# Reading the moving operand of the square layers in 16-byte runs, with tokens mixed between the two layers

## The chip, the cores and the metric

The kernel runs on one core of one Trainium2 chip. The metric is the device time of one execution in microseconds (us); lower is better. A core has TensorE for matrix products (PE in the profile, its weight loads PEld), VectorE (DVE), ScalarE (ACT), GpSimd (POOL) and SyncE (SP), which here issues nearly all DMAs. SBUF is the on-chip memory of 128 partitions, PSUM the small memory into which TensorE writes.

## The reference, cut to what matters

The input x is 32 sequences of 128 tokens with 256 features. A cross attention with a masked context comes first; then this feed-forward block, with a residual around it:

```python
def _L0_ffn_ref(x, w1_w, w1_s, w2_w, w2_s, h1_w, h1_s, h2_w, h2_s, w3_w, w3_s):
    def _tlin(x, w, s):
        return jnp.einsum('bsi,oi->bso', x, w) * s
    h = jax.nn.silu(_tlin(x, w1_w, w1_s)) * _tlin(x, w2_w, w2_s)   # 256 -> 1024, twice
    h = jax.nn.gelu(_tlin(h, h1_w, h1_s), approximate=False)       # 1024 -> 1024, square
    h = jax.nn.gelu(_tlin(h, h2_w, h2_s), approximate=False)       # 1024 -> 1024, square
    return _tlin(h, w3_w, w3_s)                                    # 1024 -> 256
x = x + _L0_xattn_ref(ctx_2048, _layernorm(x), ...)
x = x + _L0_ffn_ref(_layernorm(x), ...)
```

Each token goes through the block by itself. The weights of the block are -1, 0 or 1, and the scales s stand behind the product. So it does not matter in which order the tokens of a tile stand, as long as every element of an intermediate is treated alike and the order is restored before the last product.

## The kernel before

The 32 sequences are worked in 16 tiles of two sequences, T = 256 tokens each (`TILES`, `NB`, `T`). An intermediate of the feed-forward block lies with its features on the partitions: `hAh` and `hAl` are 128 partitions x 8 blocks of features (index k) x 256 tokens. The first 128 tokens of such a row of 256 are one sequence, the last 128 the other. Each activation is held as two parts, a rounded high part (`hAh`, `hBh`, `x2h`) and the rest (`hAl`, `hBl`, `x2l`), both of type float32r, and each product is made with both parts and summed in PSUM. Weights of the block are held as float32r in `W1`, `W2`, `H1`, `H2`, `W3`.

In a tile, TensorE makes in this order: the gate and up products (`gate_up`, four groups q of 0 to 3), the k, q and v projections of a later tile (`project_k`, `project_q`, `project_v`), the first square layer (`middle`, q of 4 to 7), attention, scores and output projection of later tiles (`attend`, `scores`, `out_proj`), the second square layer (`middle`, q of 8 to 11), and the last product (`ffn_out`, line 740). The order is written out by hand in `gates_part` and `middle_part`, and a loop runs over tiles 1 to 12.

The square layers are what the change touches. `middle_steps` works one block of 128 output features: for each of the 8 blocks k of input features it calls `part_product` twice, with the high and with the low part. In `part_product` the weights (128 x 128) are the stationary operand and a whole row of 256 tokens, `part[:, k, :]`, is the moving operand; the result goes to 256 columns of one half of a PSUM bank. That is 8 output blocks x 8 k x 2 parts = 128 matmuls for a square layer of one tile, 256 for both, 4,096 in the kernel. `ffn_group`, for the gate and up products, calls the same `part_product`; these matmuls therefore bear the same line, 627.

The first square layer (q < 8) reads `hAh`, `hAl`, the second reads `hBh`, `hBl`. Behind each group, ScalarE applies the gelu with a scale for each partition (`gelu`, line 863: PSUM to `g`), and VectorE splits `g` into the two parts (`split`, lines 1265 and 1267) for the next layer. The second layer's results are written to `hAh`, `hAl` again, which `ffn_out` reads as stationary operand, 128 tokens at a time, so that its output has tokens on partitions in their true order.

The program holds each of these paths twice: with float32r operands (`general` false) and with plain float32 ones. The weights here are exact in float32r, so the first is executed, the `return` at line 627.

Two more uses of a moving operand matter below. `project_q` reads from tile 3 on (line 496) the tile `xnT` in the order in which a DMA left it: as j, a, i with i of 32 tokens, hence in 8 runs of 32 float32 elements (128 bytes) for 256 columns. For tiles 0 to 2 (line 499) the same product reads `xnT` as one run of 256. Both write 256 PSUM columns.

By the sizes of the tiles allocated ahead of them, `hAh` begins at byte 182,944 of a partition and `hBh` at 199,328, both multiples of 32; `hAl` and `hBl` follow 8,192 bytes behind. Each run of 4 elements of the change begins at a multiple of 16 bytes.

Of the kernel before, what the change touches and what calls it, by code (L numbers as in the profile page):

```python
# [5 lines left out]
F32, F32R, I32 = mybir.dt.float32, mybir.dt.float32r, mybir.dt.int32  # L6
# [7 lines left out]
T = NB * P  # L14
TILES = B // NB
KD, KC, KH = D // P, DC // P, HID // P
# [5 lines left out]
EARLY = 2 * KD  # L22
WARM = 8
PAD = 8
MASKED = -3.0e38


# [13 lines left out]
def program(nc, x, ctxT, mask_row, mask_col, wsT, wvT, wtT, woT, first_rows, second_rows, x_mask_1, w1T, w2T, h1T, h2T,  # L41
            w3T, out):
    st = ExitStack()
    with st:
        def sb(name, shape, dt=F32):
            return st.enter_context(nc.sbuf_tensor(name, shape, dt))
# [56 lines left out]

        sb("pad", [P, PAD])
        x2h, x2l = sb("x2h", [P, KD, T], F32R), sb("x2l", [P, KD, T], F32R)
# [4 lines left out]
        y = sb("y", [P, NB, D])  # L110
# [12 lines left out]
        def mrow_of(a):  # L123
            return mrow_1 if isinstance(a, int) and a == 1 else mrow
# [36 lines left out]
        def mid_bank(f, q):  # L161

            if q in (6, 10) and isinstance(f, int) and (f == TILES - 1 or f in (0, TILES - 2) and q == 6):
                return G[0][:].rearrange("p (h t) -> p h t", h=2)
            return F[q % 2][:]
# [96 lines left out]
        def at(name, tile, k):  # L262

            value = tile * PER[name] + k
            return max(value, 0) if isinstance(value, int) else value
# [25 lines left out]
        def wait_mrow(engine, a):  # L291

            if isinstance(a, int) and a == 0:
                engine.wait_ge(firsts_loaded, 16)
            elif isinstance(a, int) and a == 1:
                engine.wait_ge(x_loaded_1, 16)
            else:
                engine.wait_ge(mrow_loaded, at("mrow_loaded", a - 2, 16))
# [148 lines left out]
        def _(pe):  # L447
            mm = nc.tensor.matmul
# [171 lines left out]
                        ins = mm(G[1][:, j * D:(j + 1) * D], lhsT, WO[:, k, :], start=k == 0, stop=k == 2 * KD - 1)  # L620
                ins.then_inc(o_done, 2)

            def part_product(bank, W, k, cols, part, first, last, general):

                if general:
                    return mm(bank, W[1][:, k, cols], part[:, k, :].bitcast(F32), start=first, stop=last)
                return mm(bank, W[0][:, k, cols], part[:, k, :], start=first, stop=last)  # L627

            def ffn_group(bank, W, cols, hi, lo, general, ready=None):

                kk = W[0].shape[1]
                for k in range(kk):
                    if ready is not None:
                        ready(k)
                    part_product(bank, W, k, cols, hi, k == 0, False, general)
                    ins = part_product(bank, W, k, cols, lo, False, k == kk - 1, general)
                return ins
# [49 lines left out]
            def middle_steps(f, q, half, ks, general):  # L687

                W, hi, lo = ((H1, H1_raw), hAh, hAl) if q < 8 else ((H2, H2_raw), hBh, hBl)
                m = 2 * (q % 4) + half  # L690
                for k in ks:
                    if m == 0 and k % 2 == 0:
                        pe.wait_ge(h_ready, at("h_ready", f, q - 4 + k // 2 + 1))
                    cols = slice(m * P, (m + 1) * P)
                    part_product(mid_bank(f, q)[:, half, :], W, k, cols, hi, k == 0, False, general)
                    ins = part_product(mid_bank(f, q)[:, half, :], W, k, cols, lo, False, k == KH - 1, general)
                if half and ks[-1] == KH - 1:
                    ins.then_inc(mid_done, 1)

            def middle(f, q, half, general):  # L700

                if half == 0 and q in (4, 8) and isinstance(f, int) and f == 0:
                    pe.wait_ge(chunk_cast, EARLY + (q // 4) * KH)
                    if q == 8 and general:
                        pe.wait_ge(raw_loaded, 112)
                if half == 0:
                    middle_bank(f, q)
                middle_steps(f, q, half, range(KH), general)

            def middle_three(f, q, general):  # L710

                three = (q, q + 1, q + 2)
                for ks in (range(4), (4, 5), (6, 7)):
                    for i in three:
                        if ks[0] == 0:
                            middle_bank(f, i)
                        middle_steps(f, i, 0, ks, general)
                for i in three:
                    middle_steps(f, i, 1, range(KH), general)
# [296 lines left out]
        def _(dve):  # L1016
# [28 lines left out]
            def mask_bias(a):  # L1045

                wait_mrow(dve, a)
                V.tensor_scalar(mbias[:], mrow_of(a), 0.0, MASKED, ALU.is_equal, ALU.mult).then_inc(mask_bias_ready, 1)

# [510 lines left out]
```

## Time and profile before

| | us |
|---|---|
| device time, median of 2 runs (907.35 to 907.44) | 907.39 |
| span of the profiled execution | 906.1 |
| TensorE busy in the span | 900.6 (99%) |
| TensorE weight loads busy | 865.1 (95%) |
| VectorE busy | 615.8 (68%) |
| ScalarE busy | 390.9 (43%) |
| GpSimd busy | 76.9 (8%) |

How to read it: the profile records one execution. Its span goes from the first to the last instruction, the device time is 1.3 us more. Busy time is the union of the instructions of an engine; matmuls overlap their neighbours, because each has a record of 0.28 us while a new one starts every 0.12 us. So the mean duration of a matmul is not what it costs; what counts is the distance from one start to the next. The granted clock (1.00 is all of it) is what the chip lets TensorE have of its 2.4 GHz.

### The profile page before, as it was taken

The page shows a single profiled execution, that of the slowest core. Times are in us where ns is not written, and L with a number is a line of the kernel's source. Part 1 is how long each engine was busy: PE and PEld are TensorE (multiplying, and loading weights), DVE is VectorE, ACT ScalarE, POOL GpSimd, SP SyncE. Part 2 cuts the span into 40 slices and gives each one's busy share as a digit, 9 for nine tenths or more (in the row PEclk, how much of TensorE's full clock was granted, in tenths as well). Part 3 has the DMA queues.
Part 4 walks back from the last instruction along what each step waited for, and adds up shares of the span by engine and source line. Part 5 has one row for each costly group of instructions (what it writes and reads, how often), then busy time and mean ns, then how long its engine had stood idle before and what let it go on. Part 6 is the DMA issues. An engine that isn't in the chain of part 4 may idle for free.

```text
span 906.1 us, 20825 instructions
## 1 busy us (share of the span) xinstructions
PE 900.6 (99%) x7600; PEld 865.1 (95%) x7600; DVE 615.8 (68%) x1224; ACT 390.9 (43%) x1100; POOL 76.9 (8%) x101
## 2 busy tenths in 40 slices
PE   9999999999999999999999999999999999999998
PEld 8899999999999999999999999999999999999998
DVE  5887858577585776857667586675857857576453
ACT  5872534435253252623525235253443524355231
POOL 3543000010000100001010010100001000000000
PEclk9999999999999999999999999999999999999999
DMA  9932132412314232142311424113241221303000
GB/s 350 382 114 58 60 88 69 122 52 78 84 46 122 58 98 64 40 122 69 112 45 35 122 69 122 35 50 106 69 122 46 72 84 59 94 24 106 24 13 14
DMA packets 82352, 79.27 MB, mean 87 GB/s; under 512 B 8592, under 2 KB 74896, under 8 KB 82320
## 3 DMA queue, kind: packets, MB, share of 16 engines
q1 hardware_dynamic: 81744, 78.31, 28.2%
q10 hardware_dynamic: 576, 0.52, 0.2%
q8 instruction: 21, 0.34, 0.2%
q14 instruction: 11, 0.09, 0.0%
HBM read 51.55 MB, written 27.26 MB: 87 GB/s over the span
## 4 chain that ended last, share of the span: by engine, by line
PE 96%; DVE 1%; DMA 1%; issue 0%; SPq 0%; POOL 0%; ACT 0%; DVEq 0%; POOLq 0%; ACTq 0%
PE F L627 56%; PE G L627 8%; PE F L740 7%; PE G L620 6%; PE G L478 6%; PE G L514 5%; PE G L496 2%; PE S L531 2%; PE G L603 2%; PE F L514 1%; PE S L467 1%; DMA cT<-ctx_t 0%; DMA p_dram<-pb 0%; DMA pr<-p_dram 0%; DVE pr L1107 0%
## 5 line engine op out<-in xcount | busy, mean ns | idle before, releaser
L863 ACT ACTIVATE g<-F,firsts 128x256 f32<-128x256 f32 x248 | 104.0, 472 | 322.9 <-PE F L627 322.7
L627 PE MATMUL F<-hBh,H 128*128 128x256 f32 x1008 | 239.2, 282 | 0.1
L627 PE MATMUL F<-hBl,H 128*128 128x256 f32 x1008 | 236.2, 279 | 0.0
L627 PE MATMUL F<-hAh,H 128*128 128x256 f32 x976 | 231.7, 282 | 0.0
L627 PE MATMUL F<-hAl,H 128*128 128x256 f32 x976 | 228.8, 279 | 0.0
L627 PEld LDWEIGHTS F<-hBl,H 128*128 128x128 f32 x1008 | 190.0, 189 | 0.4
L627 PEld LDWEIGHTS F<-hBh,H 128*128 128x128 f32 x1008 | 188.9, 187 | 0.6 <-ACT g L863 0.3
L627 PEld LDWEIGHTS F<-hAl,H 128*128 128x128 f32 x976 | 183.9, 188 | 0.3
L627 PEld LDWEIGHTS F<-hAh,H 128*128 128x128 f32 x976 | 183.0, 187 | 1.0 <-ACT sil L856 0.4
L1265 DVE CAST hBh<-g 128x512 fp32r<-128x512 f32 x64 | 28.4, 444 | 118.0 <-ACT g L863 117.8
L891 ACT ACTIVATE pr<-pr,nmx 128x128 f32<-128x128 f32 x240 | 92.7, 388 | 0.2
L1267 DVE TENSOR_TENSOR hAl<-g,hAh 128x512 fp32r<-128x512 f32 x128 | 88.7, 693 | 4.4
L1265 DVE CAST hAh<-g 128x512 fp32r<-128x512 f32 x128 | 54.9, 429 | 43.6 <-ACT g L863 42.5
L1431 POOL TENSOR_TENSOR rs<-ve,neg_half 128x2 f32<-128x2 f32 x15 | 10.4, 693 | 648.6 <-DVE ve L1202 648.6
L627 PE MATMUL F<-x2h,W 128*128 128x256 f32 x256 | 61.5, 280 | 0.0
L627 PE MATMUL G<-x2h,W 128*128 128x256 f32 x256 | 61.4, 280 | 0.0
L627 PE MATMUL F<-x2l,W 128*128 128x256 f32 x256 | 61.3, 279 | 0.0
L740 PE MATMUL F<-W,hAh 128*128 128x256 f32 x256 | 61.3, 281 | 0.0
L627 PE MATMUL G<-x2l,W 128*128 128x256 f32 x256 | 61.3, 279 | 0.0
L740 PE MATMUL F<-W,hAl 128*128 128x256 f32 x256 | 61.2, 280 | 0.0
L863 ACT ACT_TABLE_LOAD x17 | 21.8, 1283 | 76.7 <-PE F L627 76.7
L514 PE MATMUL G<-WV,cT 128*128 128x256 f32 x224 | 50.6, 379 | 0.0
(160 smaller groups left out, 1520.0 us busy)
## 6 DMA issues: line engine op xcount, KB each, us to landing
p_dram<-pb SPq DMA_DIRECT2D x30, 512.0 KB, 3.3
pr<-p_dram SPq DMA_DIRECT2D x120, 128.0 KB, 3.2
H_raw<-h SPq DMA_DIRECT2D x16, 512.0 KB, 13.8
cT<-ctx_t SPq DMA_DIRECT2D x14, 512.0 KB, 3.6
x_dram<-xt SPq DMA_DIRECT2D x28, 256.0 KB, 2.4
out<-y SPq DMA_DIRECT2D x32, 128.0 KB, 1.7
x_in<-x_t SPq DMA_DIRECT2D x15, 256.0 KB, 2.7
x2T<-x_dram SPq DMA_DIRECT2D x60, 64.0 KB, 2.0
```

The source lines that it names most:

```text
L478: ins = mm(k_part(a, c), WK[:, k, c * P:(c + 1) * P], cT_of(a)[:, k, :], start=k == 0, stop=k == KC - 1)
L496: ins = mm(to.rearrange("p (j a i) -> p j a i", j=NB, a=ROWS), WQ[:, k, c * P:(c + 1) * P], turned(xnT)[:, :, k].rearrange("p a j i -> p j ...
L514: ins = mm(v_bank(a)[:, j * D:(j + 1) * D], cT_of(a)[:, k, j * P:(j + 1) * P], WV[:, k, :], start=k == 0, stop=k == KC - 1)
L531: ins = mm(S[:, r, j, c, :], qT[rows, c, j * P:(j + 1) * P], kT[rows, c, j * P:(j + 1) * P], start=True, stop=True)
L603: ins = mm(to.rearrange("p (t b) -> p t b", t=ROWS), v[:, j, h * DH:(h + 1) * DH], pT[j][:, :, r * KD + c, :], start=True, stop=True)
L620: ins = mm(G[1][:, j * D:(j + 1) * D], lhsT, WO[:, k, :], start=k == 0, stop=k == 2 * KD - 1)
L627: return mm(bank, W[0][:, k, cols], part[:, k, :], start=first, stop=last)
L740: ins = mm(F[j][:, 0, :], lhsT, W3[:, k, :], start=first, stop=last)
L863: fn(g[:, q % 2, m, :], mid_bank(f, q)[:, m, :], ACT.Gelu, scale=scols[:, col:col + 1]).then_inc(gelu_ready, 1)
L891: ins = fn(pr[j][:, r, c, :], pr[j][:, r, c, :], ACT.Exp, bias=nmx[:, j, h:h + 1], scale=SCALE, accum_out=den[:, j, h:h + 1])
L1265: V.tensor_copy(hi[:, pair, :], g[:, q % 2, :, :]).then_inc(hi_ready, 1)
L1267: V.tensor_tensor(lo[:, pair, :], g[:, q % 2, :, :], hi[:, pair, :].bitcast(F32), ALU.subtract).then_inc(h_ready, 1)
```

## The change

The two square layers read the same 256 tokens of the same row, in another order. The constant `RUN` = 4 is new. In the first square layer the row is seen as 2 halves (b) of 32 runs (a) of 4 elements (c), and read as a, b, c: 4 tokens of the first half, 4 of the second, the next 4 of the first, and so on, with a step of 512 bytes between halves. The PSUM columns are written in order, so that in `g`, `hBh` and `hBl` the tokens of both sequences alternate in groups of 4. In the second square layer the row is seen as 32 pairs (a) of 2 runs (b) of 4 elements, and read as b, a, c: every other run of 16 bytes, first the even ones, then the odd ones. This puts the tokens back into their true order. Each of the 4,096 matmuls of the square layers thus has a moving operand of 64 runs of 16 bytes in place of one run of 1,024 bytes. The PSUM operand is rearranged to the same shape, but its addresses stay consecutive. The number of instructions, their order, the waits, the DMAs, the work of the other engines and the gate and up products stay as they are.

```diff
+RUN = 4
...
-            def part_product(bank, W, k, cols, part, first, last, general):
+            def part_product(bank, W, k, cols, part, first, last, general, order=None):
+                moving = part[:, k, :]
+                if order is not None:
+                    moving = moving.rearrange(order, a=T // (2 * RUN), b=2)
+                    bank = bank.rearrange("p (x y c) -> p x y c", x=moving.shape[1], y=moving.shape[2])
                 if general:
-                    return mm(bank, W[1][:, k, cols], part[:, k, :].bitcast(F32), start=first, stop=last)
-                return mm(bank, W[0][:, k, cols], part[:, k, :], start=first, stop=last)
+                    return mm(bank, W[1][:, k, cols], moving.bitcast(F32), start=first, stop=last)
+                return mm(bank, W[0][:, k, cols], moving, start=first, stop=last)
...
             def middle_steps(f, q, half, ks, general):
                 W, hi, lo = ((H1, H1_raw), hAh, hAl) if q < 8 else ((H2, H2_raw), hBh, hBl)
+                order = "p (b a c) -> p a b c" if q < 8 else "p (a b c) -> p b a c"
...
-                    part_product(mid_bank(f, q)[:, half, :], W, k, cols, hi, k == 0, False, general)
-                    ins = part_product(mid_bank(f, q)[:, half, :], W, k, cols, lo, False, k == KH - 1, general)
+                    part_product(mid_bank(f, q)[:, half, :], W, k, cols, hi, k == 0, False, general, order)
+                    ins = part_product(mid_bank(f, q)[:, half, :], W, k, cols, lo, False, k == KH - 1, general, order)
```

## Rows read from the trace of the kernel before

**Rows 1.** The page's head and first part: busy time, share, instructions of each engine

```profile
span 906.1 us, 20825 instructions
## 1 busy us (share of the span) xinstructions
PE 900.6 (99%) x7600; PEld 865.1 (95%) x7600; DVE 615.8 (68%) x1224; ACT 390.9 (43%) x1100; POOL 76.9 (8%) x101
```

**Rows 2.** Granted TensorE clock of the core, and waits of TensorE in all

```profile
core 0: 906.1 us, clock 1.000
...
PE G L603 <- DMA pr<-p_dram: 1.1, 2, 0.8
PE F L814 <- DVE upd L1372: 1.1, 1, 1.1
```

**Rows 3.** The page's part 4: the chain that ended last, by engine and line

```profile
PE 96%; DVE 1%; DMA 1%; issue 0%; SPq 0%; POOL 0%; ACT 0%; DVEq 0%; POOLq 0%; ACTq 0%
PE F L627 56%; PE G L627 8%; PE F L740 7%; PE G L620 6%; PE G L478 6%; PE G L514 5%; PE G L496 2%; PE S L531 2%; PE G L603 2%; PE F L514 1%; PE S L467 1%; DMA cT<-ctx_t 0%; DMA p_dram<-pb 0%; DMA pr<-p_dram 0%; DVE pr L1107 0%
```

**Rows 4.** The chain in order of time, one tile: start, length (us), line, matmul records

```profile
320.86 1.87 PE F L627 x16
322.73 3.45 PE G L478 x16
326.18 1.73 PE G L496 x8
327.91 3.45 PE G L514 x16
331.36 14.93 PE F L627 x128
346.29 1.01 PE G L603 x32
347.30 1.10 PE S L531 x32
348.40 3.65 PE G L620 x16
352.05 14.94 PE F L627 x128
366.99 3.78 PE F L740 x32
```

**Rows 5.** Timeline of TensorE: q projection with one run, between its neighbours

```profile
46.92 1.89 PE L499 MATMUL G<-xnT,WQ 128*128 128x256 f32 x8
48.64 0.38 PE L514 MATMUL G<-WV,cT 128*128 128x256 f32 x1
```

**Rows 6.** Groups of TensorE, shapes apart: count, busy us, mean ns, idle before

```profile
L627 PE MATMUL F<-hBh,H 128*128 128x256 f32 x1008 | 239.2, 282 | 0.1
L627 PE MATMUL F<-hAh,H 128*128 128x256 f32 x976 | 231.7, 282 | 0.0
L627 PE MATMUL G<-hAh,H 128*128 128x256 f32 x48 | 11.6, 280 | 0.0
L627 PE MATMUL G<-hBh,H 128*128 128x256 f32 x16 | 3.9, 278 | 0.0
```

**Rows 7.** Timeline of weight loads in the second square layer: each start is one load

```profile
299.77 0.19 PEld L627 LDWEIGHTS F<-hBh,H 128*128 128x128 f32 x1
...
300.94 0.19 PEld L627 LDWEIGHTS F<-hBh,H 128*128 128x128 f32 x1
```

**Rows 8.** The costliest groups behind the square layers on ScalarE and VectorE

```profile
L863 ACT ACTIVATE g<-F,firsts 128x256 f32<-128x256 f32 x248 | 104.0, 472 | 322.9 <-PE F L627 322.7
L1267 DVE TENSOR_TENSOR hAl<-g,hAh 128x512 fp32r<-128x512 f32 x128 | 88.7, 693 | 4.4
L1265 DVE CAST hBh<-g 128x512 fp32r<-128x512 f32 x64 | 28.4, 444 | 118.0 <-ACT g L863 117.8
```

## The prediction, made before the changed kernel ran

> **What bounds the kernel now.** I read the head of the page first: TensorE is busy for 900.6 of 906.1 us, the next engine for 68% [rows 1]. Then the clock and TensorE's waits: the granted clock is 1.000, which is the 2.4 GHz level, and the two waits listed come to 2.2 us [rows 2]. So nobody keeps TensorE waiting, and its clock has nothing to regain. The chain of waits says the same from the other side: 96% of what sets the end is TensorE work, 56% under line 627 into bank F alone [rows 3]. A busy TensorE only tells that matmuls overlap, so the view that prices them is the chain in order of time, with the length of each stage and its number of records [rows 4]. The first square layer of a tile is the stage of 128 matmuls at 331.36, 14.93 us long; the second is the stage at 352.05, 14.94 us. The next stage starts where each ends. That is 14.94/128 = 116.7 ns from start to start. The two layers of 16 tiles are 16 x (14.93 + 14.94) = 478 us, 53% of the span. Whatever one changed matmul costs more is paid 4,096 times with nothing over it: 1 ns is 4.1 us, or 0.45%.
>
> The count 4,096 is that of the groups: with the high parts alone 1,008 + 16 in the second layer and 976 + 48 in the first, 2,048 in all, and as many with the low parts [rows 6].
>
> **What a matmul is limited by today.** 256 columns at 2.4 GHz are 106.7 ns. The float32 products show how near a stream comes to that: each makes two records, and 16 of them in a row take 3.45 us, 215.6 ns a record, so that 107.8 ns for 256 columns is the pace if a record streams its columns twice (my reading of 215.6 against 2 x 106.7) [rows 4]. The float32r matmul takes 116.7 ns, 8.9 ns more. Weight loads start at the same distance: ten of them in 300.94 - 299.77 = 1.17 us, 117 ns each [rows 7]. The rows do not tell whether the load or the moving operand sets the 116.7. The gate and up stage with other tiles has the same 1.87/16 = 116.9 ns, the last product, with weights and moving operand from other places again, 3.78/32 = 118.1 ns [rows 4]. So the distance hardly depends on where the operands lie: 1.4 ns is the largest difference seen.
>
> **The change part by part.** It removes nothing and adds no instruction, wait or DMA. The gelu and the split work on whole rows with one scale per partition, whatever the order of the tokens, so their cost stays. The result is written to consecutive PSUM columns as before. The gate, up and last products are not touched. What is left is one price, p: what 64 runs of 16 bytes in place of one run of 1,024 bytes add to the distance of 116.7 ns. The change is worth 4,096 x p.
>
> No row shows p, since no moving operand in this trace has runs of 16 bytes. The nearest is the q projection. It reads 8 runs of 128 bytes from tile 3 on and one run before. The stage with 8 runs takes 1.73 us for 8 records, 216.3 ns each; its neighbours with one run take 3.45/16 = 215.6 ns [rows 4]; the same product with one run takes 48.64 - 46.92 = 1.72 us, 215.0 ns [rows 5]. The difference of 0.7 to 1.3 ns is what the rounding to 0.01 us makes of 8 records. Over 8 runs it is 0.16 ns a run at the most, and could be nothing. These rows have two weaknesses: their matmuls need 256 elements in 216 ns, half the pace of the float32r ones, and a run in them is 8 times longer. They speak against a fixed cost of restarting the address pattern, and say little on whether the memory delivers 16 useful bytes at a time fast enough.
>
> Bounds. Below: if the 8.9 ns over a bare stream were due to the order of reading and all went away, p = -8.9 ns, -36 us. Against it speaks that 116.7 ns is the same for different tiles, which looks like a property of the pair of load and matmul. Above, by cost per run: 64 x 0.16 = 10.2 ns, of which 8.9 ns may be hidden if the load sets the pace (p = 1.3 ns, +5 us), or none (+42 us). Above, by pace: if each 16-byte run costs as much as 32 bytes, 256 columns take 2 x 107.8 = 215.6 ns, p = 98.9 ns, +405 us for both layers. I take p = 0: it is the value to which the q projection is nearest, and a contiguous row must also be fetched piece by piece, so that the number of useful bytes fetched per matmul is the same; only a piece wider than 16 bytes, or a preference for neighbouring pieces, makes a difference. The runs begin at multiples of 16 bytes, so none straddles two such pieces.
>
> The trace shows 8 non-contiguous runs at 216.3 against 215.6 ns [rows 4]. The Trainium skill (Advanced Engine Details and Errata, SBUF Cachelines) says that SBUF has lines of 16 bytes and that a line needs at least two hits for full performance. Each line gets four hits here, so that by the page the sum would be the same 907 us, as with p = 0. No row of this trace tests a line of that size.
>
> Sum: 906.1 + 4,096 x 0 + 1.3 (the median less the span) = 907.4 us. Nothing comes late, so no stall moves. If p were positive, TensorE would only be later everywhere; ScalarE waits 322.9 us in front of the gelus already and VectorE 118.0 us in front of the split of `hBh` [rows 8], so these engines would wait longer, and no other bound would appear. That also means that no slack elsewhere covers p.
>
> **The rivals.**
> Both layers at half pace, 0.13. The memory delivers pieces of 32 bytes or more to TensorE, and a run of 16 bytes uses half of one. Both orders waste the other half: the first layer leaves for the other half of the row, the second steps over it. 907.4 + 405 = 1,312 us. For it: the float32r stream is the fastest reader in this kernel, 1,024 bytes in 107.8 ns, and its need has no reserve in any row. Against it: the rows with 128-byte runs, weakly.
>
> The Trainium skill says of PSUM that any non-contiguous pattern slows matmuls significantly (Advanced Engine Details and Errata, PSUM Cachelines). The PSUM side stays contiguous here; carried over to reading, the rule would be this rival. The q projection, at 216.3 against 215.6 ns, does not follow it [rows 4].
>
> One layer only at half pace, 0.11. Either the second (a step of 32 bytes always meets the same part of an interleaved memory) or the first (a jump of 512 bytes at each run, two places open at once). 2,048 x 98.9 = 203 us, 1,110 us. Nothing in the rows speaks for either; it decides as soon as the delay is over 8.9 ns or, if there is no reserve, over 0.
>
> A bubble at each run, 0.07. One period of 0.42 ns (2.4 GHz) x 64 = 26.7 ns, less 8.9 of reserve or none: p = 17.8 to 26.7, +73 to +109 us. One of 0.83 ns: p = 44 to 53, +182 to +218 us. So 980 to 1,125 us. The 0.16 ns a run above speaks against it.
>
> Faster, 0.03. The alternation relieves a collision between the reads of moving operand and weights; in full -36 us, 871 us. It passes 2% from p = -4.4 ns on. Against it is the equal distance across tiles.
>
> No effect, because the operand is read through a buffer or the load sets the pace: that is inside the forecast. The forecast itself, p between -1.4 and +4.5 ns (-6 to +18 us), has 0.66.
>
> **How the numbers follow.** Most likely 907.4 us; that case's own range is 901 to 926 us. 2% of 907.4 is 18 us, about what a measurement of this kernel can tell from no change: faster ends at 889, slower starts at 926. Faster 0.03, within 2% 0.66, slower 0.13 + 0.11 + 0.07 = 0.31. To hold 8 in 10 the range must take in a part of the slow cases: up to 1,115 us it holds the forecast, the one-layer case and nearly all bubbles, and leaves out both layers at half pace and the gain, 0.16 together. Low end: 900 us, the forecast's 6 us of gain and a little noise.
>
> **What would show it.** In the chain in order of time the two stages of 128 matmuls stay at 14.9 us. If both read 27.6 us, it is the half pace; if one does, its order names the cause. 17.2 to 18.4 or 20.6 to 21.8 us is a bubble at each run. The stages of the gate, the projections and the last product keep their lengths in every case; if they changed, the price would not be in the moving operand. In the group table the idle time before the gelus grows by about what the square layers gain in length. A granted clock below 1.000 would make the forecast wrong in a way that no step here considers.

## The result, and the profile after

The changed kernel takes 928.75 us (928.5 to 928.99, 2 runs) against 907.39 us. The ratio is 1.0235 with an interval of 1.0205 to 1.0265: slower, by a little more than 2%. The forecast was no change, 907.4 us.

The chain of waits of the changed kernel in order of time, one tile (start, length in us, engine and line, matmul records), answers to [rows 4]:

```profile
326.54 1.87 PE F L632 x16
328.41 3.45 PE G L479 x16
331.86 1.73 PE G L497 x8
333.59 3.45 PE G L515 x16
337.04 16.21 PE F L632 x128
353.25 1.01 PE G L604 x32
354.26 1.10 PE S L532 x32
355.37 3.65 PE G L621 x16
359.02 15.08 PE F L632 x128
374.10 3.78 PE F L746 x32
```

Two stages changed and no other. The first square layer, which reads in turn from both halves, went from 14.93 to 16.21 us, from 116.6 to 126.6 ns a matmul. The second, which reads every other run, went from 14.94 to 15.08 us, from 116.7 to 117.8 ns. Gates, projections, attention and last product have the lengths they had. Over 16 tiles this is 16 x (1.28 + 0.14) = 22.7 us; the span grew by 21.1 us, from 906.1 to 927.2.

Most of the missing 1.6 us went into a wait that the first longer stage covered. TensorE's waits before had 1.1 us for a DMA that brings `pr` [rows 2]; both fall in the first pass over the tiles, at 68.7 and 70.2 us. The same list of the changed kernel (engine, line, what it waited for: us, times, longest) has no such row:

```profile
PE F L820 <- DVE upd L1378: 1.1, 1, 1.1
PE F L551 <- DVE pr L1161: 0.3, 1, 0.3
```

The page of the changed kernel, head and busy times, and the group of the gelus with count, busy us, mean ns and the idle time before it, answer to [rows 1] and [rows 8]:

```profile
span 927.2 us, 20825 instructions
## 1 busy us (share of the span) xinstructions
PE 922.6 (100%) x7600; PEld 887.3 (96%) x7600; DVE 617.1 (67%) x1224; ACT 390.6 (42%) x1100; POOL 76.2 (8%) x101
...
L869 ACT ACTIVATE g<-F,firsts 128x256 f32<-128x256 f32 x248 | 104.1, 472 | 338.7 <-PE F L632 338.5
```

VectorE and ScalarE did the same work in the same time: the gelus took 472 ns in both kernels, and ScalarE only waited 15.8 us longer in front of them. The granted clock was 1.000 as before. So the loss is the pace of TensorE in the two stages.

### The profile page after: what moved, and what is told of

Its sections match the earlier page's. It is cut to its first block, busy times and chain, and to the rows that moved or that the text cites. A ratio compares the mean times of both kernels' runs of the same rounds, so it can differ in the third digit from the quotient of the medians.

```text
span 927.2 us, 20825 instructions
## 1 busy us (share of the span) xinstructions
PE 922.6 (100%) x7600; PEld 887.3 (96%) x7600; DVE 617.1 (67%) x1224; ACT 390.6 (42%) x1100; POOL 76.2 (8%) x101
## 4 chain that ended last, share of the span: by engine, by line
PE 98%; DVE 1%; issue 0%; ACT 0%; DVEq 0%; ACTq 0%
PE F L632 59%; PE G L632 8%; PE F L746 7%; PE G L621 6%; PE G L515 5%; PE G L479 5%; PE G L497 2%; PE S L532 2%; PE G L604 2%; PE S L468 0%; PE F L820 0%; DVE mx L1130 0%; DVE pr L1123 0%; PE G L500 0%; PE S L500 0%
## 5 line engine op out<-in xcount | busy, mean ns | idle before, releaser
L632 PE MATMUL F<-hAh,H 128*128 128x256 f32 x976 | 250.9, 295 | 0.0
L632 PE MATMUL F<-hAl,H 128*128 128x256 f32 x976 | 248.3, 292 | 0.0
```

What stands on the lines that cost most here:

```text
L632: return mm(bank, W[0][:, k, cols], moving, start=first, stop=last)
```

## The experiments

All are read by the length of the two stages of 128 matmuls in the chain in order of time, in a tile of the loop. Divided by 128 it is the distance from one matmul to the next. The lengths repeat from tile to tile within 0.02 us, unless the text says otherwise. Each run's kernel is the changed kernel with the edit shown; only the last one is the kernel before with its edit. Each was run once, the last one four times. The granted clock was 1.000, in the run with single elements and in the last one 0.998 on the average: it read 0.96 between 60 and 100 us and 1.00 in all later stretches, where the stages shown lie.

Four theories are asked about first. A: TensorE pays for each jump back, where the outer loop of the address pattern moves on. B: it pays for the distance between one run and the next. C: the price belongs to the place in the tile. D: the reads of weights and of the moving operand collide.

### Does the price belong to the order or to the layer

The row is split into x parts of y runs and read in turn from the parts, y times. 2 parts are the order of the first layer of the changed kernel, 32 parts that of the second, and the run swaps them:

```diff
-                    moving = moving.rearrange(order, a=T // (2 * RUN), b=2)
+                    moving = moving.rearrange("p (x y c) -> p y x c", x=order, c=RUN)
...
-                order = "p (b a c) -> p a b c" if q < 8 else "p (a b c) -> p b a c"
+                order = 32 if q < 8 else 2
```

> The two orders change places: the first square layer reads every other run (step 32 bytes), the second reads in turn from both halves of the row (step 512 bytes); the result is the same. In the changed kernel the stages of 128 matmuls took 16.21 us (126.6 ns each) in the first layer and 15.08 us (117.8 ns) in the second. If the price belongs to the order (theory A or B), the first stage takes 15.08 us and the second 16.21 us, span 927. If it belongs to the place in the tile, to what other engines do meanwhile or to the buffers hA (theory C), they stay at 16.21 and 15.08 us.

Measured, the chain in order of time:

```profile
337.77 15.07 PE F L632 x128
352.85 1.01 PE G L604 x32
353.86 1.10 PE S L532 x32
354.96 3.65 PE G L621 x16
358.61 16.23 PE F L632 x128
```

The two lengths changed places to 0.02 us, and the device time was 930.35 us. The price belongs to the order of reading. What else goes on in the tile, which buffer is read and which weights are loaded have no part in it: theory C is out.

### Jumps back, or distance

The next three runs keep 64 runs of 16 bytes in each matmul. Two have other numbers of parts, and the other layer undoes the order:

```diff
+                    moving = moving.rearrange("p (x y c) -> p y x c", x=order, c=RUN)
...
+                order = 4 if q < 8 else 16
```

and in the second run:

```diff
+                order = 8 if q < 8 else 8
```

> The row is seen as 4 quarters of 16 runs, the first layer reads in turn from the four quarters (steps of 256 bytes, 15 jumps back); the second undoes it (16 parts of 4 runs, steps of 64 bytes, 3 jumps back). Still 64 runs of 16 bytes in each matmul. Theory A, a price for each jump back or change of the outer index (31 of them cost 9.9 ns, 0.32 ns each): 116.7 + 4.8 = 121.5 ns, 15.55 us in the first layer, 117.7 ns, 15.06 us in the second. Theory B, a price for each far step: the first layer has 48 steps of 256 bytes and 15 of 752, no fewer than before, so 126 ns, 16.2 us; the second, with 64-byte steps, between 15.08 and 16.2 us.

> The row is seen as 8 parts of 8 runs and both layers read in turn from the 8 parts (steps of 128 bytes, 7 jumps back), which undoes itself. Theory A: 116.7 + 7 x 0.32 = 118.9 ns, 15.2 us in both layers. Theory B: as many steps of 128 bytes as the first layer of the changed kernel has of 512, so well above 15.2 us in both, up to 16.2, if 128 bytes are far.

The third keeps the nest of loops of the first layer, 32 steps of 16 bytes and in each a pair of runs, but brings the pair near. Each bracket is [step, count] in elements of 4 bytes, the outermost loop first:

```diff
+                moving = bass.AP(moving.tensor, moving.offset, [moving.ap[0], *order])
...
+                order = [[4, 32], [8, 2], [1, 4]] if q < 8 else [[4, 32], [32, 2], [1, 4]]
```

> Both square layers read 32 pairs of runs of 16 bytes, as the first layer of the changed kernel does, with the same 32 steps of 16 bytes of the outer index, but the two runs of a pair lie only 32 bytes apart in the first layer and 128 bytes apart in the second, instead of 512. Some tokens are read twice and others not at all, so the output is not the reference's; the work is the same. Theory A (price for each jump back or change of the outer index): both layers at 126.6 ns, 16.2 us. Theory B (price for distance): the first near 117.8 ns, 15.1 us, the second between that and 16.2 us.

Measured, the stages of 128 matmuls. The run with 4 and 16 parts:

```profile
339.58 17.09 PE F L632 x128
...
362.44 14.69 PE F L632 x128
```

The run with 8 parts in both layers:

```profile
340.13 16.24 PE F L632 x128
...
362.13 15.82 PE F L632 x128
...
397.84 15.83 PE F L632 x128
```

The run with near pairs:

```profile
335.01 15.47 PE F L637 x128
...
356.25 15.37 PE F L637 x128
```

Neither theory holds. In ns a matmul: 2 parts 126.6, 4 parts 133.5, 8 parts 123.6 or 126.9, 16 parts 114.8, 32 parts 117.8, and as pairs 512 bytes apart 126.6, 128 bytes apart 120.1, 32 bytes apart 120.9. With 4 parts there are half as many jumps back as with 2, and the price is higher, so theory A is out. With near pairs it lies between the values of A and B, but the nearer pair is no cheaper than the farther, and 32 parts with steps of 32 bytes cost less than pairs at 32 bytes, so distance alone is out too. Two things were not expected. Eight parts have two lengths for the same instructions, 15.83 and 16.24 us, in turn from tile to tile in the first layer; the second layer, with the same order, always has the shorter. What alternates was not found. And 16 parts, 114.8 ns, are faster than one run, 116.7 ns: the one run of the kernel before is no floor.

### Collisions with the weight load

Two runs ask for theory D. In the first, the square layers' weight loads read one element over and over; in the second, the moving operands lie 32 bytes lower and the weights stay.

> Each weight load of the square layers reads one and the same element of a partition 128 times (step 0) in place of 128 elements; the output is not the reference's, the number and shape of instructions stays. The first layer reads its moving operand as one run (116.6 ns in the kernel before), the second in turn from four quarters, steps of 256 bytes, as the first layer of the run with 4 and 16 parts did (133.5 ns there). Theory D, the reads of weights and of the moving operand collide in the memory and the order only changes how often: both layers come to one distance, near the 107.8 ns of the bare stream, 13.8 us a stage. Theory E, the moving operand alone pays for its far steps: the first layer 14.9 us as before or a little less, the second still about 2.1 us longer than the first.

```diff
+                weights = bass.AP(weights.tensor, weights.offset, [weights.ap[0], [0, P]])
...
+                order = [[1, 256]] if q < 8 else [[4, 16], [64, 4], [1, 4]]
```

> The changed kernel with the pad of 32 bytes ahead of x2h taken out, so that all moving operands of the block (x2h, x2l, hA, hB) lie 32 bytes lower, at a multiple of 64 in place of 32 over one, while the weights stay. Theory D with parts of the memory chosen by low address bits: the stages differ from 16.21 and 15.08 us in at least one layer by over 0.1 us. Theory E: both stay.

```diff
-PAD = 8
+PAD = 0
...
-        sb("pad", [P, PAD])
```

The run with fixed weights, second layer of one tile and first layer of the next two:

```profile
305.32 17.15 PE F L639 x128
...
342.36 15.36 PE F L639 x128
...
400.52 14.52 PE F L639 x128
```

The second and third rows are the first layer, with one run. It has two lengths in turn from tile to tile, as the eight parts had: of the 13 stages of the chain seven took 15.36 us (120.0 ns) and six 14.51 or 14.52 us (113.4 ns). Their mean, 14.97 us, is within 0.04 us of the 14.93 us with real weights. The layer with four parts took 17.15 us, 134.0 ns, against 133.5 with real weights. A weight load that always reads the same element does not remove the cost, so theory D in its plain form is out: most of what the four parts cost does not depend on which addresses the weight load reads. But the one run became 3.4 ns slower in some tiles and 3.3 ns faster in others, so the addresses that the weight load reads are not without effect: with one run a collision of some kind is not excluded.

The run without the pad, a stage of 16 gate products and the two layers:

```profile
321.87 1.92 PE G L631 x16
...
338.18 16.20 PE F L631 x128
...
360.15 15.08 PE F L631 x128
```

With all moving operands 32 bytes lower, at multiples of 64, the two changed layers stayed at 16.20 and 15.08 us, as theory E expected, by which the moving operand alone pays. But the gate products, which read one run, went from 1.87 to 1.92 us for 16, from 116.9 to 120.0 ns. So where a single run starts matters by 3 ns a matmul, and the two orders of the change do not feel it. Whether its own address matters or its place against the weights is open: with fixed weights a single run took the same 120.0 ns in seven stages at its old address.

The two lengths also say how far a comparison of orders carries. One order, and even one run, can differ by up to 6.6 ns a matmul for a reason that was not found. The 126.6 ns of 2 parts and 117.8 ns of 32 were met in both layers, and 4 parts twice at 133.5 and 134.0 ns; 16 parts and each of the near pairs have only one layer of one run.

### What sets 116.7 ns, the load or the columns

> Both square layers read their moving operand as one run, of 224 columns in the first and 128 in the second in place of 256; the remaining tokens are left out, so the output is not the reference's. If the weight load alone sets the 116.7 ns: both stages stay at 14.9 us. If the stream of columns does: 224/256 and 128/256 of it, 102 and 58 ns, 13.1 and 7.5 us. If a load needs about as long as 256 columns do (107 ns) and the rest of 116.7 ns is collision: 107 to 112 ns in the second layer, 13.7 to 14.3 us, whatever the columns.

```diff
+                order = [[1, 224]] if q < 8 else [[1, 128]]
```

```profile
325.59 14.28 PE F L637 x128
...
345.64 14.24 PE F L637 x128
```

224 columns take 111.6 ns and 128 columns 111.2 ns. At both sizes the pair of weight load and matmul needs this distance: the floor. It is not a cost of issuing a pair, for the 32 of line 603, with weight loads of 32 columns, take 1.01 us, 31.6 ns each [rows 4]. With 256 columns in one run the distance is 116.7, 5 ns above the floor. So in the kernel before it is the moving operand that sets the pace, and nothing that is added to its reading is hidden. By its numbers this is the third case of the expectation, 13.7 to 14.3 us whatever the columns. Its reason, that the rest of 116.7 ns is a collision with the load, is not shown, and the next run speaks against a collision paid once a load.

The next run tells whether this is paid for each matmul or for each column. Each matmul gets 512 columns. The first layer reads two whole rows of `hA`; the second reads pairs of runs 512 bytes apart, which covers three quarters of two rows of `hB`, some of it twice:

```diff
+                    moving = part[:, k - k % 2, :]
...
+                order = [[1, 512]] if q < 8 else [[4, 64], [128, 2], [1, 4]]
```

> Each matmul of the square layers reads 512 columns, two rows of hA or hB, and writes both halves of the bank: twice the work on other tokens' columns, so the output is not the reference's. The first layer reads one run of 512; the second reads runs of 16 bytes in turn from two places 512 bytes apart, as the first layer of the changed kernel does, 128 runs. If the 8.9 ns over the bare stream of 256 columns, and the 10.0 ns that this order added, are paid once for each matmul: 222 to 225 ns in the first layer (28.5 to 28.8 us), 232 to 235 in the second (29.7 to 30.1 us). If they are paid for each run or piece: 233 ns (29.9 us) and 253 ns (32.4 us).

The chain, second layer of one tile and first of the next:

```profile
348.81 31.58 PE F L638 x128
...
400.28 29.87 PE F L638 x128
```

One run of 512 columns takes 233.4 ns, twice 116.7. The 8.9 ns over the bare stream of 256 columns are therefore no fixed cost of a matmul; they are its pace, 0.456 ns a column. This pace is that of a run with these weights and addresses, since with fixed weights some stages were faster (113.4 ns for 256 columns). The pairs take 246.7 ns, 13.3 more for 128 runs, where 64 runs cost 10.0 more: neither once a matmul nor quite in proportion. This part fits neither of the two expectations (the two kernels' rows do not have the same places, which may be why).

### Shorter runs

> Runs of one element (4 bytes) in place of 4: the first layer reads in turn one element from each half of the row, the second every other element (step 8 bytes); the result is the same. If memory is fetched in pieces of 16 bytes of which each access of another piece costs a fetch, the first layer makes 256 fetches in place of 64: the column pace halves at least, over 213 ns, 27 us or more; the second makes two hits on each piece, 128 fetches: between 15 and 27 us. If the order of the bytes matters only through collisions with the weight load: both between 14.7 and 17.1 us.

```diff
-RUN = 4
+RUN = 1
...
+                    moving = moving.rearrange("p (x y c) -> p y x c", x=order, c=RUN)
...
+                order = 2 if q < 8 else 128
```

```profile
194.56 14.29 PE F L632 x128
208.86 1.01 PE G L604 x32
209.87 1.10 PE S L532 x32
210.97 3.65 PE G L621 x16
214.62 29.29 PE F L632 x128
```

This is the most telling pair. Single elements taken in turn from two places 512 bytes apart take 111.6 ns, the floor: faster than one run, and 15.0 ns faster than 16-byte runs from the same two places. Single elements with a step of 8 bytes take 228.8 ns, twice the pace. So it is not the number of jumps that costs. Neither expectation holds in either layer: fetches wanted 27 us or more in the first and 15 to 27 in the second, collisions 14.7 to 17.1 us in both, and it was 14.29 and 29.29 us. The collisions are near in the first layer and far off in the second.

> The first layer reads every other run of 8 bytes (2 elements), in two passes over the row; the second reads single elements with a step of 16 bytes, in four passes. The results are not put in order, so the output is not the reference's. Theory F, TensorE fetches pieces of 16 bytes, at best one in 1.67 ns (64 pieces in 107 ns), and every piece left and met again is fetched again: 128 pieces in the first layer, 228 ns as with every other element, 29.3 us; 256 pieces in the second, 427 to 460 ns, 55 to 59 us. Theory G, two hits on a piece are enough for the full pace and only something about the inner step of 8 bytes cost 228.8 ns: 15 us in the first layer, more in the second.

```diff
+                order = [[2, 2], [4, 64], [1, 2]] if q < 8 else [[1, 4], [4, 64]]
```

The chain, second layer of one tile and first of the next:

```profile
342.19 29.86 PE F L637 x128
...
391.94 29.29 PE F L637 x128
```

Runs of 8 bytes with a step of 16 take 228.8 ns, the same as single elements with a step of 8. Single elements with a step of 16 bytes, which use a quarter of each 16-byte piece, take 233.3 ns and not the 427 that a limit on pieces asks for. Theory F met the first layer (29.3 us) and fails in the second, theory G fails in the first: the pace halves and then stays there.

> The first layer reads element by element in turn from four quarters of the row (step 256 bytes), the second from its eight eighths (step 128 bytes). The results are not put in order, so the output is not the reference's. With two halves the stage took 14.29 us. If TensorE keeps four or more pieces of 16 bytes open: 14.3 us in the first layer; eight: 14.3 us in the second too. Where it keeps fewer than the order needs, each element is a fetch: 256 pieces, 427 to 460 ns, 55 to 59 us.

```diff
+                order = [[1, 64], [64, 4]] if q < 8 else [[1, 32], [32, 8]]
```

```profile
341.17 18.33 PE F L637 x128
...
365.26 28.16 PE F L637 x128
```

Four places in turn, element by element, take 143.2 ns and eight places 220.0 ns. Two places are free (111.6 ns), four are dear, eight come near the half pace. Neither expected value came out.

A rule that fits most of this: it is as if TensorE took two float32r elements at a time, and the elements with even and those with odd numbers in the stream behave like two readers, each of which wants two of its own elements in a row from one 16-byte piece. One run gives each reader exactly two. 16-byte runs in any order do too: 114.8 to 133.5 ns, never the half pace. Singles from two halves give each reader four in a row, and only here is the floor of 111.6 ns reached. A step of 8 bytes, 8-byte runs with a step of 16, and a step of 16 bytes all give one: 228.8, 228.8 and 233.3 ns. Four and eight places give one in a row but return to the same pieces at once, and lie between. The rule says nothing of the differences among 16-byte runs, 114.8 to 134.0 ns, which is where the change's own price lies. It was formed behind the runs and no run was made to break it, so it is an argument and not shown.

The Trainium skill (Advanced Engine Details and Errata, SBUF Cachelines) wants two hits on a 16-byte line for full performance. Taken for the whole stream, the runs differ: a step of 8 bytes has two hits on a line and takes 228.8 ns against 116.7.

### Single elements from both halves in every layer

Here the order that reached the floor is used in the gate, up and both square products of the kernel before, and undone where `g` is written:

> Gate, up and both square layers read their moving operand element by element in turn from both halves of the row (steps of 512 bytes), and the tokens are put back at once: the gelu and the gate times up write g with the same steps. The result is the same. With runs of one element the first square layer took 14.29 us (111.6 ns), the same as with 224 columns, against 14.93 before. If that holds in each place: 14.3 us in both square layers and 1.79 us in place of 1.87 for 16 gate or up products, 5,120 x 5.0 = 26 us less than before, 882 us, ratio 0.971. If the strided writes of g cost ScalarE and VectorE so much that TensorE waits, or if the gain needs the other layer's order, between 890 and 907 us.

```diff
-                moving = part[:, k, :]
...
+                moving = part[:, k, :].rearrange("p (b a) -> p a b", b=2)
+                bank = bank.rearrange("p (a b) -> p a b", b=2)
...
+                    fn(g[:, q % 2, m, :].rearrange("p (b a) -> p a b", b=2),
+                       mid_bank(f, q)[:, m, :].rearrange("p (a b) -> p a b", b=2), ACT.Gelu,
...
+                    V.scalar_tensor_tensor(g[:, q % 2, p % 2, :].rearrange("p (b a) -> p a b", b=2),
...
```

It took 901.11 us (899.87 to 901.89, 4 runs) beside 907.98 us of the kernel before (7 runs, taken together with it), ratio 0.992 with an interval of 0.9903 to 0.9936: 0.8% less, clear of the noise and less than half of the 2% that is called a change here. The chain of one tile, a wait of TensorE, the gelu, and the gate times up in this kernel (lowest, median and highest ns) and, last, in the kernel before (busy us and mean ns):

```profile
331.10 14.29 PE F L629 x128
...
351.16 14.29 PE F L629 x128
365.45 3.95 PE F L742 x32
369.40 1.80 PE G L629 x16
...
371.93 0.66 DVE g L1249
...
PE G L478 <- DVE g L1249: 8.2, 13, 0.6
...
L865 ACT ACTIVATE g<-F,firsts 128x256 f32<-128x256 f32 x248 | 148.3, 706 | 278.6 <-PE F L629 278.4
...
L1249 DVE SCALAR_TENSOR_TENSOR g<-G,firsts,sil x64: 631/666/691, 37.6 to 862.0; 128x256 f32<-128x256 f32 x64
...
L1246 DVE SCALAR_TENSOR_TENSOR g<-F,firsts,sil 128x256 f32<-128x256 f32 x64 | 27.9, 478 | 10.4 <-PE F L627 10.4
```

Both square layers reach the floor, which is 16 x (14.93 + 14.94 - 28.58) = 20.6 us. The 64 stages of 16 gate or up products, at 1.80 in place of 1.87 us, add 4.5 us. Of these 25 us the device time kept 6.9; nearly three quarters were given back. The gate times up with steps of 512 bytes in its output takes a median of 662 to 666 ns, where its mean was 478 ns in the kernel before (median 476 to 477), and now stands on the chain between the gate groups: `project_k` alone waited 8.2 us for it. The gelu takes 706 in place of 472 ns, and the last product 3.95 in place of 3.78 us for 32. The version that suggests itself, this order in the square layers alone, with gate and up as they were, was not run.

## Where the prediction was wrong, and where it was right

The range of 900 to 1,115 us holds 928.75 us. The most likely value, 907.4 us, is 21 us below it, that case's own range of 901 to 926 us ends below it, and the direction, with 0.66 on within 2%, was missed. That the range holds it is luck in part: it was made wide for one layer at half pace and for a bubble at each run, and neither came.

**The bound and the exchange rate held.** TensorE is the bound, 4,096 matmuls are changed, 1 ns on each is 4.1 us, nothing but a wait of about 1 us at the start covers it, and nothing else becomes late. (10.0 + 1.1) x 2,048 = 22.7 us is the change by this rate, and the span grew by 21.1 us.

**The term that failed is p = 0.** It was the price of reading 64 runs of 16 bytes in place of one run, and it measured 10.0 ns in the first layer and 1.1 ns in the second, 5.6 on the average. The prediction had the price in its bounds: 0.16 ns a run, what rounding allowed in the q projection, times 64 is 10.2 ns, and with no reserve +42 us if both layers paid it [rows 4, 5]. I took the other end, since the difference of 0.7 to 1.3 ns could be rounding. That a bound of 0.16 ns a run is small in the q projection and 9% of a float32r matmul with 64 runs should have widened the likeliest case's range to 949 us and moved chance from within 2% to slower. That the number came out near 10.2 is no proof of a price for each run, for single elements in turn made 256 runs at no cost at all. The bound itself rests on one of two readings of the float32 records that exclude each other. Where the prediction takes 107.8 ns as the pace, a record passes its columns twice; where it takes 8 runs for a record and calls them half the pace, it passes them once. With two passes it is 16 runs a record and the bound 1.3/16 x 64 = 5.2 ns, which the first layer exceeded. No run tells which holds.

**The reserve was not there.** The prediction left open whether load or columns set 116.7 ns, and let 8.9 ns be hidden if it was the load. The run with fewer columns puts the floor of the pair at 111.2 to 111.6 ns, below. The moving operand sets the pace, by 5 ns, and in the run with 512 columns it is 0.456 ns a column. The bare stream of 107.8 ns, taken from float32 records, was not the pace of a float32r run.

**"Hardly depends on where the operands lie" was too strong.** It rested on 1.4 ns between three stages [rows 4]. All three had operands laid out with the pad; without it the gate products cost 3 ns more, and with fixed weights one run took 113.4 or 120.0 ns.

**The rivals.** The half pace is real, 228.8 to 233.3 ns, but was met only with runs of 8 and 4 bytes and not with 16; the argument that a row must be fetched piece by piece anyway was good for that. That only one layer would pay much was nearest to what came, the first 10.0 ns and the second 1.1, but by a tenth of the price that this rival had. The bubble at each run is out as a mechanism. The collision with weight reads, the place where a gain could come from, was put at -36 us against the mark of -8.9 ns; the most that an order gained is 5.1 ns, 20.6 us, which ends at the floor of the pair. Whether it came by a relieved collision is open, since the fixed weights moved the one run both ways.

**What stays open.** Why 16-byte runs from 2 and 4 parts cost 10 and 17 ns, from 16 parts -1.9 ns, and why 8 parts, and one run with fixed weights, have two lengths in turn. So the cause of the price that the change paid is not found. That the price goes with the order of the addresses and not with the number of jumps is shown; which part of the memory is met twice is not. The rule of two readers is untested.

## What to carry to other kernels

Before a new price is set to zero, multiply the resolution of the nearest row by the count it will have: 0.16 ns a run was nothing on 8 runs and 10 ns on 64. Ask of a matmul stream first which of load and columns sets the distance, by a run with fewer columns; only then is it known whether a slower read is hidden. For float32r moving operands keep at least 16 contiguous bytes, or take single elements from two places: the first avoids the half pace, but 16-byte runs still cost between 1.9 ns less and 17 ns more than one run. Both ends of such a rearrangement must be priced, since the strided write of 256 elements cost ScalarE 234 ns and VectorE 185 to 190 ns more. And compare the same stage over many tiles before a few ns are put down to an order, since the same instructions can have two lengths.

## What the runs showed of the hardware that was not expected

- One contiguous float32r run is not the fastest order: 116.7 ns for 256 columns, against 111.6 ns for single elements in turn from two places 512 bytes apart and 114.8 ns for 16-byte runs from 16 parts.
- A weight load of 128 columns with its matmul takes 111.2 ns with 128 moving columns and 111.6 ns with 224.
- A start 32 bytes lower, at a multiple of 64 bytes, with the weights where they were, makes a single run 3 ns slower (120.0 against 116.9 ns) and leaves the two orders of 16-byte runs as they are.
- Steps of 8 and of 16 bytes cost nearly the same, 228.8 and 233.3 ns, twice the pace of one run.
- The same instructions had two steady lengths in turn from tile to tile: 123.6 and 126.9 ns with 8 parts, 113.4 and 120.0 ns with one run and fixed weights.
